# V's weight rows in places of their own, a stage border without waits for transfers, and x1 and z loaded over used halves of the Q and K weights

## What is computed

```python
x = x + xattn(layernorm(x), ctx_2048, wq, wk, wv, wo)          # x1 of the kernel
# self attention, 16 heads of 128, on x1
Q = einsum('btc,ncd->btnd', xn, W_Q) + b_Q                      # K and V in the same way
Q, K = rope(Q), rope(K)
probs = softmax(where(causal, Q @ K.T / sqrt(128), -inf))
z = probs @ V
x = x + einsum('bqnd,ndm->bqm', z, W_O) + b_O                   # the merge
h = silu(gate) * up                                             # weights decoded from 4 bits
x = x + rms(h @ W_down)
```

## Time and profile before

| what | value |
|---|---|
| time of the kernel, median of 3 runs | 1384.15 us (1381.96 to 1385.51) |
| the profiled execution: its time, its span | 1385.5 us, 1383.7 us |
| PE busy | 1340.2 us (97%) |
| DVE busy | 1005.3 us (73%) |
| ACT busy | 508.6 us (37%) |
| POOL busy | 380.9 us (28%) |
| granted TensorE clock, mean | 0.988 |

### The profile page before, as it was taken

The page is one execution under the profiler, slowest core; times in us unless marked ns, Lnnn a source line. Parts: engine busy times, 40 slices in busy tenths (PEclk is TensorE's granted clock), DMA queues, the critical chain, the costliest instruction groups (busy, mean ns, idle before and its releaser), DMA issues. The chain is left out here.

```text
span 1383.7 us, 23386 instructions
## 1 busy us (share of the span) xinstructions
PE 1340.2 (97%) x9216; PEld 777.6 (56%) x9216; DVE 1005.3 (73%) x2285; ACT 508.6 (37%) x1252; POOL 380.9 (28%) x302
## 2 busy tenths in 40 slices
PE   8999999967999999999999999999899999999998
PEld 6666666634666666666666666654344434434443
DVE  6444444257888888898888887856999698688684
ACT  3222222232343433433343433330001386666671
POOL 0000000002222222222222122211133296748571
PEclk9999999989999999999999999999999999999999
DMA  8555544613110022011101021077761000000001
GB/s 336 206 199 198 202 187 183 228 65 122 32 32 25 23 63 62 31 32 59 49 32 31 32 62 32 19 197 215 189 213 61 1 1 1 0 1 31 1 31 61
DMA packets 36902, 122.56 MB, mean 89 GB/s; under 512 B 4281, under 2 KB 4921, under 8 KB 28089
## 3 DMA queue, kind: packets, MB, share of 16 engines
q1 hardware_dynamic: 36520, 118.19, 25.2%
q10 hardware_dynamic: 272, 2.88, 0.8%
HBM read 95.89 MB, written 25.17 MB: 87 GB/s over the span
## 5 line engine op out<-in xcount | busy, mean ns | idle before, releaser
L871 POOL TENSOR_TENSOR hd_rotated<-hd_products 64x512 f32<-64x512 f32 x32 | 40.3, 1259 | 742.5 <-DVE hd_products L1122 742.5
L191 PE MATMUL psum<-hd_xt_hi,hqk_hi 128*128 128x512 f16 x512 | 194.6, 380 | 1.6 <-DVE hd_xt_lo L1096 1.6
L192 PE MATMUL psum<-hd_xt_lo,hqk_hi 128*128 128x512 f16 x512 | 194.3, 379 | 0.0
L193 PE MATMUL psum<-hd_xt_hi,hqk_lo 128*128 128x512 f16 x512 | 194.3, 379 | 0.0
L1508 POOL TENSOR_TENSOR ff_part<-ff_part 128x512 f32<-128x512 f32 x88 | 129.9, 1479 | 83.1 <-DVE ff_part L1640 82.9
L1640 DVE SCALAR_TENSOR_TENSOR ff_part<-psum,gu_scale,ff_part 128x512 f32<-128x512 f32 x176 | 123.0, 742 | 36.4 <-PE psum L1534 30.7
L191 PE MATMUL psum<-hd_wv_hi,hd_xt_hi 128*128 128x256 f16 x512 | 140.3, 274 | 4.5 <-DVE hd_wv_lo L1101 4.5
L192 PE MATMUL psum<-hd_wv_lo,hd_xt_hi 128*128 128x256 f16 x512 | 140.4, 274 | 0.0
L193 PE MATMUL psum<-hd_wv_hi,hd_xt_lo 128*128 128x256 f16 x512 | 140.4, 274 | 0.0
L1533 PE MATMUL psum<-ff_xt_hi,gu 128*128 128x512 f16 x352 | 134.4, 382 | 5.4 <-DVE ff_part L1640 4.8
L1534 PE MATMUL psum<-ff_xt_lo,gu 128*128 128x512 f16 x352 | 134.2, 381 | 0.0
(11 more groups left out here) (188 smaller groups left out, 3004.4 us busy)
## 6 DMA issues: line engine op xcount, KB each, us to landing
xa_kv_t<-in_ctx_t_dram SPq DMA_DIRECT2D x16, 1024.0 KB, 5.4
xa_kv<-in_ctx_dram SPq DMA_DIRECT2D x16, 1024.0 KB, 4.9
w_rows<-in_head_weights_dram SPq DMA_DIRECT2D x12, 1024.0 KB, 7.8
z_scratch<-hd_z_hi SPq DMA_DIRECT2D x32, 256.0 KB, 2.6
z_scratch<-hd_z_lo SPq DMA_DIRECT2D x32, 256.0 KB, 3.3
w_rows<-z_scratch SPq DMA_DIRECT2D x8, 1024.0 KB, 8.6
hqk_lo<-z_scratch SPq DMA_DIRECT2D x8, 1024.0 KB, 7.1
xn<-in_x_dram SPq DMA_DIRECT2D x8, 512.0 KB, 4.0
```

The costliest lines, as they stand in the source:

```text
L191: pe.matmul(out, lh, rh, start=(first and i == 0), stop=False)
L192: pe.matmul(out, lh, rl, start=False, stop=False)
L193: last = pe.matmul(out, ll, rh, start=False, stop=(final and i == k - 1))
```

## The change

It has three parts. **The border.** SP no longer waits at the end of the cross attention block. The semaphores `rows_loaded` and `x1_stored` move to the caller, and whoever needs the transfers waits in the heads phase: ScalarE, VectorE and SP wait for the stores of x1 at their start (the new buffers lie where x1 lay), and ScalarE waits for blocks 0 and 1 of V ahead of splitting them. **V's blocks 2 and 3** get places of their own: block 3 goes over `rotated`, block 2 over `xn` once the transposes have read it. GpSimd's first sum and the next load of `xn` therefore wait for `w_lo_done`. VectorE clears `pt_hi` and `pt_lo` at its start. **x1 and z over used weights.** The host orders the columns of Q and K by pair, so pairs 0 to 3 of the heads fill the first half of each row of `hqk`. After pair 3 of the last tile is projected, SP loads x1 of tiles 0 and 1 and the second half of z of tile 0 over that half (`load_first_halves`); x1 of tile 1 is not loaded in the merge any more. Codes, scales and shifts go over the second half, in pieces of 352 numbers with gaps; b_O gets a buffer of its own.

```diff
@@ xattn_phase, end of SP's stream
-            for n in range(2):
-                sp.wait_ge(x1_stored[n], 32 * (NH // 2))
-            for i in range(2):
-                sp.wait_ge(rows_loaded[i], 16 * (2 + (NH + 2) // 2))
@@ heads_phase
+        def wait_x1_stored(eng):
+            for n in range(2):
+                eng.wait_ge(x1_stored[n], 32 * (NH // 2))
+
+        wv_rows = [w_rows[:, 0, :], w_rows[:, 1, :], xn[:, :, :].rearrange("p b d -> p (b d)"),
+                   rotated[:, :, :, :].rearrange("p a b t -> p (a b t)")]
...
+            wait_x1_stored(sp)
+            load_rows(3)
             for dst, src in ((cos, rope_cos), (sin, rope_sin), (mask, causal)):
...
-            for k in range(2, KD):
-                sp.wait_ge(w_lo_done, k - 1)
-                sp.dma_start(w_rows[:, k % 2, :], head_weights[(2 * KD + k) * P:(2 * KD + k + 1) * P, :]).then_inc(loaded[k % 2], 16)
+            for k in range(KD):
+                banks.wait_filled(sp, {}, ("x", k))
+            load_rows(2)
...
             def load_for_merge(last_proj):
                 banks.wait_filled(sp, last_proj, ("k", 1))
-                for half in range(2):
-                    sp.dma_start(early.second_z[half], z_of(z_scratch, half, 1, 0)).then_inc(early_sems.z_loaded, 16)
...
-                sp.dma_start(early.x2[:, 0:TT, :], rows_of(0)).then_inc(early_sems.x1_loaded, 16)
+            def load_first_halves(last_proj):
+                banks.wait_filled(sp, last_proj, ("k", 1))
+                for t in range(2):
+                    sp.dma_start(early.x2[t], rows_of(t * TILE)).then_inc(early_sems.x1_loaded, 16)
+                for half in range(2):
+                    sp.dma_start(early.second_z[half], z_of(z_scratch, half, 1, 0)).then_inc(early_sems.z_loaded, 16)
...
+                if s.last_tile and s.pair == PAIRS // 2 - 1:
+                    load_first_halves({"turn": NT, "proj": s.a})
...
-                cols = slice(pair * DH + half * (WIDE // 2), pair * DH + half * (WIDE // 2) + DH)
+                cols = slice((2 * pair + half) * DH, (2 * pair + half + 1) * DH)
@@ ScalarE, VectorE of heads_phase
+            wait_x1_stored(act)
             first_halves({})
             for k in range(KD):
-                if k >= 2:
-                    act.wait_ge(loaded[k % 2], 16)
-                act.activation(wv_hi[:, k, :], w_rows[:, k % 2, :], ACT.Copy, scale=WS).then_inc(w_hi_done, 1)
+                if k < 2:
+                    act.wait_ge(first_rows_loaded[k], 16 * (2 + (NH + 2) // 2))
+                else:
+                    act.wait_ge(late_rows_loaded[k], 16)
+                act.activation(wv_hi[:, k, :], wv_rows[k], ACT.Copy, scale=WS).then_inc(w_hi_done, 1)
...
+            wait_x1_stored(dve)
+            dve.memset(pt_hi[:, :, :, :], 0.0)
+            dve.memset(pt_lo[:, :, :, :], 0.0).then_inc(zeros_set, 1)
             second_halves({}, 0)
@@ merge_phase
             load_z(1, 0)
             sp.dma_start(codes[1], codes_of(gu_codes, 1)).then_inc(gu_loaded[1], 16)
-            load_x1(1)
```

More of the change, by code:

```diff
@@ L717, with __init__ @@
 class Early:
-    def __init__(self, hqk_hi, hqk_lo):
-        flat = hqk_lo[:, :, :].rearrange("p a n -> p (a n)")
-        at = [0]
-        def take(n):
-            at[0] += n
-            return flat[:, at[0] - n:at[0]]
-        half = HEADS // 2
-        self.x2 = hqk_hi[:, :, :].rearrange("p a n -> p (a n)").bitcast(F32).rearrange("p (b d) -> p b d", d=D)
-        self.second_z = tuple(take(half * TILE).rearrange("p (h t) -> p h t", t=TILE) for _ in range(2))
-        self.b_o = take(2 * D).bitcast(F32)
-        self.codes = take(2 * GU).bitcast(I32)
-        self.gu_scale_f16 = take(KD * 2 * FB)
-        self.shift = take(2).bitcast(I32)
+    def __init__(self, hqk_hi, hqk_lo, b_o):
+        rows = hqk_hi[:, :, :].rearrange("p a n -> p (a n)").bitcast(F32).rearrange("p (a h d) -> p h a d", h=2, d=D)
+        self.x2 = [rows[:, t // 2, t % 2 * TT:t % 2 * TT + TT, :] for t in range(NT)]
+        half = HEADS * DH // 2
+        first, second = (hqk_lo[:, :, i * half:(i + 1) * half] for i in range(2))
+        self.second_z = tuple(first[:, i * TT:(i + 1) * TT, :].rearrange("p a (h t) -> p a h t", t=TILE) for i in range(2))
+        n = GU // 8
+        self.codes = second[:, :, 0:2 * n].bitcast(I32)
+        self.gu_scale_f16 = second[:, 0, 2 * n:2 * n + KD * 2 * FB]
+        self.shift = second[:, 1, 2 * n:2 * n + 2].bitcast(I32)
+        self.b_o = b_o[:, :]
 class EarlySems:
@@ L760, in merge_heads @@
         head = half * n + i
-        pe.matmul(out, z_hi[:, i, at], wo_hi[:, head, :], start=(head == 0), stop=False)
-        pe.matmul(out, z_hi[:, i, at], wo_lo[:, head, :], start=False, stop=False)
-        last = pe.matmul(out, z_lo[:, i, at], wo_hi[:, head, :], start=False, stop=(head == HEADS - 1))
+        z_hi, z_lo = (a[:, i // 2, i % 2, at] for a in z)
+        pe.matmul(out, z_hi, wo_hi[:, head, :], start=(head == 0), stop=False)
+        pe.matmul(out, z_hi, wo_lo[:, head, :], start=False, stop=False)
+        last = pe.matmul(out, z_lo, wo_hi[:, head, :], start=False, stop=(head == HEADS - 1))
     return last
 def z_of(z_scratch, hi_or_lo, half, t):
-    return z_scratch[hi_or_lo, t, half, :, :, :]
+    return z_scratch[hi_or_lo, t, half, :, :, :].rearrange("d (a h) t -> d a h t", h=2)
 def heads_phase(nc, psum, ident, x1_rows, xn, stat, head_weights, hqk_hi, hqk_lo, w_rows, b_q, b_k, b_v,
                 rope_cos, rope_sin, causal, w_o, wo_hi, wo_lo, z_scratch, first_z, small_loaded_z_stored,
-                early, early_sems, b_o, shifts, gu_scales, gu_codes):
+                early, early_sems, b_o, shifts, gu_scales, gu_codes, first_rows_loaded, x1_stored):
     with ExitStack() as ctx:
@@ L808, in heads_phase @@
         z_hi, z_lo = sb("z_hi", [P, 2, TILE], F16), sb("z_lo", [P, 2, TILE], F16)
-        loaded = [sem("rows0_loaded"), sem("rows1_loaded")]
+        wo_loaded, late_rows_loaded = sem("wo_loaded"), {k: sem(f"rows{k}_loaded") for k in range(2, KD)}
         w_hi_done, w_lo_done = sem("w_hi_done"), sem("w_lo_done")
@@ L934, in step @@
                     return
+                if not s.att:
+                    pool.wait_ge(w_lo_done, KD)
                 banks.wait_moved(pool, s.runs_proj, ("q", 1))
@@ L1248, in merge_phase @@
         hi_done, lo_done, value_ready = sem("hi_done"), sem("lo_done"), sem("value_ready")
-        x1_loaded, x1_ready = {t: sem(f"x1_{t}_loaded") for t in range(1, NT)}, sem("x1_ready")
+        x1_loaded, x1_ready = {t: sem(f"x1_{t}_loaded") for t in range(2, NT)}, sem("x1_ready")
         z_loaded = [sem("z0_loaded"), sem("z1_loaded")]
@@ L1365, in decode_gu @@
                     last(dve.tensor_scalar(codes[g % 2], codes[g % 2], shift[:, 0:1], None, ALU.logical_shift_right))
-                decode_fp4(dve, last, codes[g % 2][:, at], sign[:, :], magnitude[:, :], 0)
+                decode_fp4(dve, last, codes[g % 2][:, at.start // PIECE, :], sign[:, :], magnitude[:, :], 0)
                 as_f16 = sign[:, :].bitcast(F16).rearrange("p (n two) -> p n two", two=2)[:, :, 0]
```

55 lines of the change are left out of this document (28 added, 27 removed).

## The result

The changed kernel takes 1375.17 us (median of 7 runs, 1371.99 to 1377.66) beside 1381.96 us of the kernel before on the same chip (7 runs); the ratio is 0.9924 with a 95% interval of 0.9904 to 0.9943. Applied to the median that the prediction started from (1384.15), that is 1373.6 us, against 1369 forecast. The quotient of the two medians is 0.9951 and of the two means 0.9937; the record does not say how the ratio of 0.9924 is formed, so 6.8 us (medians) to 10.5 us (ratio) of gain are all in these numbers. The change makes the kernel faster, by less than forecast. In the later runs two single executions, one of e9 (4937 us) and one of e10 (3276 us), fell far outside all others and are not in the ratios.

A forecast was written before the change was run, and what follows sets the result against it. TensorE bounds the pairs of heads; gains lie where it waits for transfers at the border and in the merge. Median 1384.15 less 15.3 us (9.8 at the border, 5.5 in the merge) gives 1368.9, rounded to 1369; range 1366 to 1375.

The forecast's parts named there:

- case (c): Rival: block 2 of V late at the border and z(1, half 1) still late in the merge, 1375 to 1379; chance 0.03.
- The border without waits: End of cross attention: without SP's wait for the last row load, TensorE starts 4.4 us earlier; waits for x1's stores hidden.
- case (f): Rival, more than forecast: block 2 comes at once (0.6 us), transposes run faster after shorter idle (1.8 us), 1366 to 1367; chance 0.08.
- V's weights: Behind the border: block 2 lands at 307.6, last low part ends at 314.0 rather than 322.86, a gain of 8.9 us.
- case (a): Rival: block 2 of V late, or border still ends with the transfers; costs 4.1 to 4.4 us, near 1373; chance 0.15.
- The clears: Ahead of the first scores: VectorE's first product with cosine no longer stands behind the two clears, 0.94 us more gained.
- Sum at the border: At the first scores: 8.9 us from V's weights plus 0.9 from the clears, 9.8 us earlier.
- The last tile: Four megabytes issued ahead of pair 3's store of z take 11 us of a pair's 18.56; cost nothing.
- The merge: TensorE's wait for z(1, half 1) and half pace behind it go: 4.1 + 1.4 = 5.5 us.
- the waits only move: Rival: nothing measurable, since TensorE meets each wait at the next instruction; 1384, chance 0.03.
- VectorE's room: In the merge VectorE waits 6.9 us for TensorE and 2.57 for codes group 1, so can be 5.5 us earlier.
- The rule on the number of engines: Codes' transfers: largest number up to 16 dividing both sides' outermost size; eight copies of 16 rows give eight engines, share 0.50.

The follow-up runs named there:

- e9: Kernel before with only codes groups 2 and 3 each cut into eight transfers of 352 columns; ratio 0.9954 against the kernel before, merge 156.54 us.
- e10: The changed kernel run again without any edit, beside the others on one chip; ratio 0.9893 against the kernel before.
- e2: Changed kernel with SP's two waits at the end of the cross attention block put back; ratio 0.9914 against the kernel before.
- e4: Changed kernel with V's block 2 over `rotated` and loaded first, block 3 over `xn`; ratio 0.9883 against the kernel before.
- e6: Changed kernel with the places of V's blocks 2 and 3 exchanged and block 3 issued ahead of the six small loads; ratio 0.9895 against the kernel before.
- e1: Changed kernel with x1 and z loaded where the kernel before loads them, keeping border, V's places and weight layout; ratio 0.9895 against the kernel before.
- e5: Changed kernel with codes group 3 as eight transfers of 352 columns on the same queue; ratio 0.9894 against the kernel before, merge 155.99 us.
- e3: Changed kernel with codes group 3 issued only once z(2, half 0) has landed; ratio 0.9886 against the kernel before, merge 155.98 us.
- e7: Changed kernel with codes' 16 rows as outer dimension, eight copies inner, groups 0 and 2 in eight transfers; ratio 0.9885 against the kernel before.

## Why the prediction was right, and where it was off

- **The number: in the range, with luck.** By the ratio the time is 1373.6 us. The sum of the events gives only 7.5 us, 1376.6, above the range of 1366 to 1375; on its own chip the changed kernel's median is 1375.17. Block 2 late and a late z together were case (c), at a chance of 0.03 and 1375 to 1379.
- **The border without waits: right.** 4.6 us at the first transpose against 4.4 forecast. The stores of x1 are what ended ScalarE's and VectorE's waits, at 295.5 and 295.7, 1.7 and 1.9 us behind the row load (forecast 1.7 to 1.8); by an estimate from the pace of the transposes (four at 0.121 us) ScalarE lost 0.15 us by them. The transposes ran at full clock (granted 1.00), 1.94 us for sixteen where they had taken 3.65 at a granted clock of 0.50; the prediction had this only in case (f), and e10 has 2.81. The half clock came later instead, in the projections:

```profile
300.00:301.00 1.00, 1.00 (x4) 0.50 0.96 387
301.00:302.00 1.00, 1.00 (x4) 0.50 1.06 326
302.00:303.00 1.00, 1.00 (x4) 0.50 1.21 386
```

The projections take 12.2 us, 10.5 before, and end at 17.7 where 16.8 was forecast; V's weights are later still and hide it. ScalarE's first split of V's weights came 3.63 us behind the row load's issue, forecast 5.3.
- **V's weights: right in kind, one term mis-sized.** The step that failed is "at the later of 302.3 + 4.8 = 307.1 and 304.8 + 2.7 = 307.5": it took the travel of two loads for that of three with six small ones among them. Counted from the issue of the last row load, block 3 was due at 7.6 us and landed at 8.8, and block 2 was due at 10.4 us and came at 12.5 (7.0 us on the way). ScalarE's wait was 4.84 us, not 1 to 1.5, beyond the 3 us that I had named as the mark of an error; of the 3.4 us too much 2.2 are the load's and 1.3 come from ScalarE being ready earlier. The low parts ended at 18.96 where 16.8 was forecast, and V's product still waited 1.32 us for them where no wait was forecast. This is half of case (a). e2 shows the overlap's price (0.68 us of waiting when two load at a time), e4 and e6 what the order and the small loads add: with both changed the low parts end at 15.35.
- **The clears: right.** From the end of the low parts to the first softmax it is 12.40 us, 13.36 before: 0.96 us, forecast 0.94. TensorE's wait ahead of the scores is 4.9 us, forecast about 5.
- **Sum at the border: less than forecast.** 7.6 us at the first softmax and 7.2 at the last store, forecast 9.8; the missing 2.2 us are block 2's.
- **The last tile: right.** Four megabytes ahead of the stores of pair 3 cost nothing; from softmax to last store no time is lost that e1, without them, does not lose too (596.0 and 596.1 us).
- **The merge: wrong, and for two reasons; this is the larger error.** "I take the wait as gone" was right for the one wait it spoke of, 5.64 us against 5.5 forecast. But the prediction never asked when z(2, half 0) is needed once TensorE is not held up ahead of it. It had 26.4 us before, since the 5.6 us of waiting fell into its time, and now has 20.7; its load takes 24 beside codes group 3. Losing the cover alone would have cost next to nothing: the load was done 20.8 us after its first issue before (0.4 us to the second issue and 20.4 to its landing), 0.1 us too late by that estimate. The other 3.3 us are the load's own, 23.7 us rather than 20.4, with codes group 3 now 3.3 us ahead of it. This alone would have fitted into 26.4 us as well; it took both. Profiles with this same order have 21.3 and 22.2 (e2, e10), 23.8 and 24.0 (e6, e4), so how much is order and how much spread is not separated. All this is "the waits only move", which the prediction weighed at the border and not here. And the reason given, x1 of tile 1 gone from the queue, is not needed: e1 has it in the queue and no wait, e9 has the old queue and no wait. Whether it would have been enough with the codes in long runs no run shows. What all runs without a wait for z(1, half 1) share is codes group 2 in short runs, and for z(2, half 0) e5 shows that, on the same half of the engines, the length of the runs decides. What was left by this error is 0.35 us of 5.5 (1.84 in e10).
- **VectorE's room: right.** It let 5.65 us through in e3 and waits for no codes.
- **The rule on the number of engines** from the Trainium skill ("DMA: Bandwidth & Descriptors", section on why a DMA increments its semaphore by 16) is borne out by e7: eight copies outside give a share of 0.57, sixteen rows outside 1.05, the rate goes from 119 to 276 GB/s. The same page's section on queues has an engine take turns packet by packet, which agrees with the packets of e5 from 978 us on, if the profile counts the same packets: four times as many of the codes, each an eighth as long, at a third of the time. It does not show in the first 4 us behind z's issue, in which the codes keep their half of the engines there too (54.7% and 54.4% from 974 to 978 us).

## What to carry to other kernels

When a wait goes, go on to the next transfer of the same kind and count its time anew: the stall had been part of its cover, and a load that was issued 26 us ahead may now be issued 21 us ahead. Ask also what is now issued ahead of it on the other queue. Load first what is needed first, and keep small loads behind large ones that something waits for. Where two queues share the engines, compare the lengths of their runs before their bytes.

## What the runs showed of the hardware

- The two transfers of z, 2 MB in runs of 8 KB, landed at a median of 19.1 us beside codes in runs of 11264 bytes (changed kernel), 10.9 us beside the same codes in runs of 1408 bytes (e5) and 5.8 us with no codes group 3 beside them (e3).
- The same 1.44 MB of codes group 2 went at 119 GB/s with eight copies as the outer dimension and at 276 GB/s with 16 rows outside, in eight transfers (e7).
- A 1 MB row load took 4.9 us (median) before; the three that overlap in the changed kernel took 5.8, 7.1 and 7.0 us, and each of the six small ones among them 5.3 to 6.1, which had taken 1.6 to 2.0. With two under way and the small ones among them it was 4.8 and 4.9 us (e2).
- Executions of one kernel differ in where TensorE runs at 1.2 GHz: behind a wait of 2.3 us at the end of cross attention it fell to 0.50 for three windows of 1 us in one profile and not in another, 1.7 us of span. Differences of 1 to 3 us could therefore only be read from event to event, and even so the pairs of heads spread over 1.5 us.
